# An expert loop on Trainium2: the next expert's input products formed between this one's output products

## The chip, the cores and the metric

The kernel runs on one core of one Trainium2 chip. The core has five engines that run by themselves and meet at semaphores: TensorE (PE, matrix products; PEld is its loading of the stationary operand), VectorE (DVE), ScalarE (ACT), GpSimd (POOL) and SyncE (SP, which here only issues transfers). The metric is device time in microseconds. Three timed runs of the kernel before gave 1420.69, 1421.56 and 1422.44 us; the median is 1421.56.

## What is computed

A decoder layer over 16 sequences of 256 tokens with 256 features: a state-space scan, an alignment with a second set of sequences, and a mixture of experts. Only the last matters here:

```python
gate_logits = jnp.einsum('te,ex->tx', x, gate_kernel)
weights, selected = jax.lax.top_k(gate_logits, TOP_K)      # 64 experts, 2 per token
...
h0 = jax.lax.ragged_dot(sorted_x, w0, group_sizes)         # 256 -> 512
h1 = jax.lax.ragged_dot(sorted_x, w1, group_sizes)         # 256 -> 512
inter = jax.nn.silu(h0) * h1
out_sorted = jax.lax.ragged_dot(inter, wo, group_sizes)    # 512 -> 256
```

4096 tokens times two choices are spread over 64 experts, each with 1.5 MB of float32 weights (w0, w1 and wo, 512 KB each).

## The kernel before

The kernel runs its stages one after the other: `states`, `wave`, `trace_back`, `expand` (which also routes the tokens), `experts` and `combine`. The change is in `experts` (line 1816) alone.

The experts are sorted by how many tokens they got. The 32 fullest are *wide*: they have room for 220 down to 134 tokens (`ROOM`, line 43), so two tiles of rows. The others are *narrow*, with room for 128. `TURN` (line 148) takes them in turns, wide, narrow, wide, and so on, 63 in all (`RANKS`); tokens that found no room, and the last expert, are served by a loop at the end (line 2003).

For expert k the work is, with m counting the four parts of 128 of the 512 hidden features:

- POOL gathers its tokens (`gather`), four experts ahead in a ring of four; PE turns them so that features lie on partitions (`turn`), and DVE copies that out of PSUM (`take_turned`, line 2042) into one of two buffers `xt`.
- PE forms part m of both input products in `h_ps[m]` (`up`, line 1942; for each of the two products two matmuls of 128 rows of features, and the float32 ones count double in the trace, so 8 records a part).
- ACT applies silu to the first (`activate`, line 2019), DVE multiplies by the second into `inter[m]` (`product`, line 2048).
- PE adds part m's share of the output product: `down` (line 1953) for a narrow expert, with 256 columns in 2 records; `down_wide` (line 1958) for a wide one, transposed, in 4 records of as many columns as tokens. For a wide expert ACT copies the result (line 2033), PE turns it back (`back`, line 1968) while it works on the next expert, and DVE takes it out (`take_out`, line 2055). POOL scatters the rows to DRAM (`scatter`).
- SP loads the weights of expert k + 4 into the slot of expert k as soon as the last output product of k is done (lines 1862 to 1864), in three transfers. Four slots (`WRING`) are there.

The order on each engine is written out by hand. On PE it is, for expert k: up 0, up 1, the turning back of the wide expert before, up 2, down 0, up 3, down 1, the turning of the tokens of k + 1, down 2, down 3 (lines 1979 to 1996). Then expert k + 1 begins. ACT does the four silus and, for a wide expert, the copy. DVE does the four products, with the taking out of the wide expert before between the second and third, then the copy of the turned tokens, then the taking out of a narrow expert.

Of the kernel before, what the change touches and what calls it, by code (L numbers as in the profile page):

```python
# [6 lines left out]
ACT = mybir.ActivationFunctionType  # L7
# [13 lines left out]
FC = F // P  # L21
# [17 lines left out]
WRING = 4  # L39
RANKS = E - 1  # L40
# [1775 lines left out]
def experts(K):  # L1816


    nc, sem = K.nc, K.sem
    XR = 4  # L1820
    with ExitStack() as c:
# [7 lines left out]
        ot = sb("mo_ot", [P, DC, 2 * P])  # L1829
# [5 lines left out]
        ot_ps = ps("mo_ot_ps", [P, DC, 2 * P])  # L1835
# [9 lines left out]
        room = [ROOM[r] for r in TURN]  # L1845
        wide = [r < WIDE for r in TURN]
# [80 lines left out]
        def _(pe):  # L1927
# [11 lines left out]
            def turn_static(k):  # L1939
                turn(k, k % XR, moved(k), room[k], wide[k])  # L1940
# [27 lines left out]
            def back(k):  # L1968
# [6 lines left out]
                                                ot[:, c_, a * P:a * P + n], K.ident[:, :])  # L1975
                m.then_inc(back_mm, 1)

            turn_static(0)
            for k in range(RANKS):
                r, n = k % WRING, room[k]  # L1980
                pe.wait_ge(K.w_in[r], (k // WRING + 1) * 48)
                go_down = down_wide if wide[k] else down
                up(k, r, k % 2, 0, n)
                up(k, r, k % 2, 1, n)
                if k >= 1 and wide[k - 1]:
                    back(k - 1)
                up(k, r, k % 2, 2, n)
                if not wide[k] and k >= 2:
                    pe.wait_ge(o_ok, k - 1)
                go_down(k, r, 0, n)  # L1990
                up(k, r, k % 2, 3, n)
                go_down(k, r, 1, n)
                if k + 1 < RANKS:
                    turn_static(k + 1)
                go_down(k, r, 2, n)
                go_down(k, r, 3, n)
                if k == RANKS - WRING + 1:
                    pe.wait_ge(down_mm, k * FC)
                    pe.sem_inc(done, 1)
            back(RANKS - 1)  # L2000
            n = late_count(pe)
            r = RANKS % WRING
            with pe.Fori(0, n) as g:
# [12 lines left out]
        @block.scalar  # L2016
        def _(act):

            def activate(k, m, n):
                act.wait_ge(up_mm, k * FC + (m + 1))  # L2020
                if not isinstance(k, int) or k >= 1:
                    act.wait_ge(inter_ok, k * FC + (m + 1 - FC))
                nc.scalar.activation(silu[m][:, 0:n], h_ps[m][:, 0, 0:n], ACT.Silu).then_inc(silu_ok, 1)  # L2023

            nc.scalar.preload_act_table(ACT.Silu)
            for k in range(RANKS):
                for m in range(FC):
                    activate(k, m, room[k])
                if wide[k]:
                    act.wait_ge(down_mm, k * FC + FC)  # L2030
                    if backs(k) > 1:
                        act.wait_ge(back_mm, backs(k) - 1)
                    nc.scalar.activation(ot[:, :, 0:room[k]], ot_ps[:, :, 0:room[k]], ACT.Copy).then_inc(ot_ok, 1)
            n = late_count(act)
            with act.Fori(0, n) as g:
                for m in range(FC):
                    activate(g + RANKS, m, P)

        @block.vector
        def _(dve):  # L2040
# [23 lines left out]
                m.then_inc(o_ok, 1)  # L2064

            take_turned(0, 0, room[0])
            for k in range(RANKS):
                for m in range(FC):
                    product(k, m, room[k])
                    if m == 1 and k >= 1 and wide[k - 1]:  # L2070
                        take_out(k - 1)
                if k + 1 < RANKS:
                    take_turned(k + 1, (k + 1) % 2, room[k + 1])
                if not wide[k]:
                    take_out(k)
            take_out(RANKS - 1)
            n = late_count(dve)
            with dve.Fori(0, n) as g:
                k = g + RANKS
# [134 lines left out]
```

## Time and profile before

| | us |
|---|---|
| median of three timed runs | 1421.56 |
| the profiled execution, timed | 1432.94 |
| its span | 1431.2 |
| PE busy | 986.7 (69% of the span) |
| DVE busy | 906.0 (63%) |
| POOL busy | 678.4 (47%) |
| ACT busy | 554.0 (39%) |

The span is cut into 40 slices of 35.8 us; the expert loop takes slices 27 to 38 or so. Busy time of PE holds the modelled length of every matmul, which in a stream overlaps the next, so a gap in PE is a little longer than its idle time. A group of the waits says which engine waited with which instruction, and what released it. SPq rows are transfers that SP issued.

### The profile page before, as it was taken

What the parts mean: (1) busy time and instruction counts of PE and PEld (TensorE: products, weight loads), DVE (VectorE), ACT (ScalarE), POOL (GpSimd) and SP (SyncE); (2) the same over time, 40 slices, a digit from 0 to 9 for tenths busy, and PEclk for the clock granted to TensorE, in tenths of its full rate; (3) what the DMA queues carried; (4) which work ended last, traced back from release to release, by engine and by line L of the source; (5) the groups of instructions that cost most, each with busy time, mean ns of one, the idle gap of its engine ahead of it and who ended that gap; (6) DMA issues with size and microseconds to landing.
All of it is one profiled execution on the core that took longest, in us unless ns stands there. A gap on an engine that the chain in (4) does not pass through costs nothing. (4 is left out here: it accounts for less than half of the span.)

```text
span 1431.2 us, 20102 instructions
## 1 busy us (share of the span) xinstructions
PE 986.7 (69%) x6433; PEld 893.7 (62%) x6433; DVE 906.0 (63%) x2024; ACT 554.0 (39%) x1236; POOL 678.4 (47%) x685
## 2 busy tenths in 40 slices
PE   3667778777788762677001675399999898989950
PEld 2566757767677651666001564399998888888850
DVE  1999999999999950888887765133323232323217
ACT  3668787786877650443000442021212121111110
POOL 5886887878778720000000677334343434444310
PEclk9989999999999985555555976599999999999985
DMA  6544545555465511122130111678788788778629
GB/s 199 180 142 139 172 139 181 157 160 181 138 183 163 167 41 38 19 41 37 22 115 34 45 45 31 204 239 268 263 271 261 258 268 265 263 252 267 220 67 349
DMA packets 171161, 231.99 MB, mean 162 GB/s; under 512 B 42172, under 2 KB 95788, under 8 KB 170352
## 3 DMA queue, kind: packets, MB, share of 16 engines
q1 hardware_dynamic: 152924, 207.06, 46.3%
q0 software_dynamic: 11280, 19.06, 4.0%
q10 hardware_dynamic: 6852, 4.57, 1.0%
q8 instruction: 52, 0.85, 0.2%
q14 instruction: 53, 0.43, 0.1%
HBM read 202.78 MB, written 23.65 MB: 158 GB/s over the span
## 5 line engine op out<-in xcount | busy, mean ns | idle before, releaser
L848 PE MATMUL st_y_ps<-ident,st_hc 128*128 128x128 f32 x2048 | 276.2, 293 | 114.2 <-DVE st_hc L491 114.1
L848 PEld LDWEIGHTS st_y_ps<-ident,st_hc 128*128 128x128 f32 x2048 | 258.5, 205 | 137.3 <-DVE st_hc L491 136.6
L373 POOL TENSOR_TENSOR st_u<-st_dx,codes 128x1024 f32<-128x1024 f32 x128 | 299.0, 2359 | 37.8 <-DVE st_h L483 37.2
L483 DVE TENSOR_TENSOR_SCAN st_h<-st_da,st_u 128x512 f32<-128x512 f32 x256 | 298.0, 1206 | 9.8 <-POOL st_u L373 9.6
L1949 PE MATMUL mo_h<-mo_xt,w 128*128 128x128 f32 (+17 forms) x2048 | 283.0, 290 | 1.8 <-DVE mo_xt L2046 1.0
L1949 PEld LDWEIGHTS mo_h<-mo_xt,w 128*128 128x128 f32 x2048 | 272.8, 194 | 6.3 <-issue 2.5
L2052 DVE TENSOR_TENSOR mo_inter<-mo_silu,mo_h 128x128 f32<-128x128 f32 (+17 forms) x256 | 75.0, 304 | 289.6 <-ACT mo_silu L2023 242.8
L1890 POOL DMA_INDIRECT outs<-mo_o,choice x95 | 93.7, 986 | 246.1 <-DVE mo_o L2063 233.9
L2023 ACT ACTIVATE mo_silu<-mo_h 128x128 f32<-128x128 f32 (+17 forms) x256 | 70.8, 290 | 327.7 <-PE mo_h L1949 227.1
L614 ACT ACTIVATE st_da<-st_delta,st_a_neg 128x510 f32<-128x510 f32 x256 | 171.7, 685 | 66.4 <-DVE st_h L483 59.6
L491 DVE TENSOR_TENSOR st_hc<-st_h,st_cps 128x1024 f32<-128x1024 f32 x128 | 152.9, 1195 | 0.0
L1083 PE MATMUL wv_e<-wv_r,wv_shift 128*128 128x1 f32 x274 | 75.8, 347 | 57.7 <-DVE wv_r L1021 57.3
L1883 POOL DMA_INDIRECT mo_xg<-xn,table x95 | 92.5, 974 | 37.6 <-issue 28.4
L1083 PEld LDWEIGHTS wv_e<-wv_r,wv_shift 128*128 128x128 f32 x274 | 68.5, 312 | 65.4 <-issue 63.9
L1963 PE MATMUL mo_ot_ps<-mo_inter,wo 128*128 128x190 f32 (+16 forms) x512 | 90.3, 310 | 23.5 <-DVE mo_inter L2052 16.2
L1963 PEld LDWEIGHTS mo_ot_ps<-mo_inter,wo 128*128 128x128 f32 x512 | 74.8, 193 | 31.4 <-DVE mo_inter L2052 21.6
L621 ACT ACTIVATE st_cps<-codes 128x512 f32<-128x512 f32 x128 | 76.6, 599 | 39.5 <-DVE st_hc L491 39.3
L1955 PE MATMUL mo_o_ps<-wo,mo_inter 128*128 128x256 f32 x256 | 73.9, 392 | 0.0
L1418 POOL DMA_INDIRECT bucket<-ex_row,ex_slot x64 | 63.1, 985 | 17.9 <-issue 17.8
L1073 ACT ACTIVATE wv_r<-wv_e,wv_edge_big 128x1 f32<-128x1 f32 x137 | 35.8, 261 | 64.7 <-PE wv_e L1083 64.7
L1147 POOL MEMSET tb_shift<- 128x128 f32 x1 | 0.2, 206 | 110.6 <-POOLq L910 110.6
L1686 ACT ACTIVATE ex_apart<-ex_col,ex_mid 128x256 f32<-128x256 f32 x32 | 14.2, 494 | 96.9 <-DVE ex_mid L1481 96.7
(300 smaller groups left out, 1332.9 us busy)
## 6 DMA issues: line engine op xcount, KB each, us to landing
codes<-bc SPq DMA_DIRECT2D x256, 256.0 KB, 3.9
w<-in_L_ffn_w_dram SPq DMA_DIRECT2D x128, 512.0 KB
wo<-in_L_ffn_wo_dram SPq DMA_DIRECT2D x64, 512.0 KB
co_got<-outs SPq DMA_DIRECT2D x16, 512.0 KB, 6.2
x<-in_x_dram SPq DMA_DIRECT2D x8, 512.0 KB, 8.9
st_cx<-in_ctx_dram SPq DMA_DIRECT2D x8, 512.0 KB, 4.4
dist<-st_dd SPq DMA_DIRECT2D x8, 512.0 KB, 5.2
codes<-wv_code SPq DMA_DIRECT2D x32, 128.0 KB, 3.4
```

The source lines that it names most:

```text
L373: nc.gpsimd.tensor_tensor(u_sb[k % URING][:, :, :], dx[p % 2][:, :, :], over_chunks(b_sb[k % BRING]), ALU.mult).then_inc(u_ok, 1)
L483: nc.vector.tensor_tensor_scan(h_sb[k % HRING][:, dh, :], da_ps[dh][:, :], u_sb[k % URING][:, dh, :], 0.0, ALU.mult, ALU.add).then_inc(h_o ...
L491: nc.vector.tensor_tensor(hc_sb[k % RING][:, :, :], h_sb[k % HRING][:, :, :], over_chunks(c_ps[k % 2][:, :]), ALU.mult).then_inc(hc_ok, 1)
L614: nc.scalar.activation(by_batch(da_ps[dh][:, :]), by_batch(delta[p % 2][:, dh, :]), ACT.Exp, scale=a_neg[:, dh, n:n + 1]).then_inc(da_ok, 1)
L621: nc.scalar.activation(c_ps[k % 2][:, :], c_sb[k % CRING], ACT.Copy).then_inc(c_ok, 1)
L848: m = nc.tensor.matmul(y_ps[t // 2][:, t % 2, dh * P:(dh + 1) * P], hc_sb[k % RING][:, dh, t * P:(t + 1) * P], K.ident[:, :], start=False, ...
L1083: nc.tensor.matmul(e_ps[t % 4][:, 0:1], K.shift[:, :], r[:, t + 1, SW:SW + 1], start=True, stop=True).then_inc(e_mm, 1)
L1883: nc.gpsimd.indirect_dma_start(xg[k % XR][0:n, a, :], None, K.xn_dram[:, :], bass.IndirectOffsetOnAxis(ap=K.table[0:n, at:at + 1], axis=0) ...
L1890: nc.gpsimd.indirect_dma_start(K.outs_dram[:, :], bass.IndirectOffsetOnAxis(ap=K.choice[0:n, at:at + 1], axis=0), o_sb[k % XR][0:n, a, :], ...
L1949: ins = nc.tensor.matmul(h_ps[m][:, i, 0:n], K.w[r][i][:, c_, m * P:(m + 1) * P], xt[u][:, c_, 0:n], start=(c_ == 0), stop=(c_ == DC - 1))
L1963: ins = nc.tensor.matmul(ot_ps[:, c_, 0:n], K.w[r][2][:, m, c_ * P:(c_ + 1) * P], inter[m][:, 0:n], start=(m == 0 and c_ == 0), stop=(m == ...
L2052: nc.vector.tensor_tensor(inter[m][:, 0:n], silu[m][:, 0:n], h_ps[m][:, 1, 0:n], ALU.mult).then_inc(inter_ok, 1)
```

## The change

PE works in iterations k = -1 to 62. In each it forms part m of the input products of expert k + 1, then part m of the output product of expert k, for m = 0 to 3. Behind m = 1 it turns back the wide expert k - 1, and behind m = 2 it turns the tokens of expert k + 2. ACT takes the transposed result of expert k - 2 ahead of the silus of expert k. DVE takes out a narrow expert k - 1 at the head of an iteration, then does the products of expert k + 1, with the taking out of a wide k - 1 behind m = 1 and the copy of the turned tokens of k + 2 behind m = 2. The slots of the weights stay four, and are freed as before by the last output product; the weights of expert k + 1 are now in use while those of k still are. The go-ahead for the weights of the last loop waits for the output products of expert 60.

```diff
+            def down_of(k, m):
+                if not wide[k] and m == 0 and k >= 2:
+                    pe.wait_ge(o_ok, k - 1)
+                (down_wide if wide[k] else down)(k, k % WRING, m, room[k])
+
             turn_static(0)
-            for k in range(RANKS):
-                r, n = k % WRING, room[k]
-                pe.wait_ge(K.w_in[r], (k // WRING + 1) * 48)
-                go_down = down_wide if wide[k] else down
-                up(k, r, k % 2, 0, n)
-                up(k, r, k % 2, 1, n)
-                if k >= 1 and wide[k - 1]:
-                    back(k - 1)
-                up(k, r, k % 2, 2, n)
-                if not wide[k] and k >= 2:
-                    pe.wait_ge(o_ok, k - 1)
-                go_down(k, r, 0, n)
-                up(k, r, k % 2, 3, n)
-                go_down(k, r, 1, n)
-                if k + 1 < RANKS:
-                    turn_static(k + 1)
-                go_down(k, r, 2, n)
-                go_down(k, r, 3, n)
+            for k in range(-1, RANKS):
+                after = k + 1
+                if after < RANKS:
+                    pe.wait_ge(K.w_in[after % WRING], (after // WRING + 1) * 48)
+                for m in range(FC):
+                    if after < RANKS:
+                        up(after, after % WRING, after % 2, m, room[after])
+                    if k >= 0:
+                        down_of(k, m)
+                    if m == 1 and k >= 1 and wide[k - 1]:
+                        back(k - 1)
+                    if m == 2 and after + 1 < RANKS:
+                        turn_static(after + 1)
                 if k == RANKS - WRING + 1:
-                    pe.wait_ge(down_mm, k * FC)
+                    pe.wait_ge(down_mm, k * FC + FC)
                     pe.sem_inc(done, 1)
-            back(RANKS - 1)
+            if wide[RANKS - 1]:
+                back(RANKS - 1)
...
-            for k in range(RANKS):
-                for m in range(FC):
-                    activate(k, m, room[k])
-                if wide[k]:
-                    act.wait_ge(down_mm, k * FC + FC)
-                    if backs(k) > 1:
-                        act.wait_ge(back_mm, backs(k) - 1)
-                    nc.scalar.activation(ot[:, :, 0:room[k]], ot_ps[:, :, 0:room[k]], ACT.Copy).then_inc(ot_ok, 1)
+
+            def take_transposed(k):
+                act.wait_ge(down_mm, k * FC + FC)
+                if backs(k) > 1:
+                    act.wait_ge(back_mm, backs(k) - 1)
+                nc.scalar.activation(ot[:, :, 0:room[k]], ot_ps[:, :, 0:room[k]], ACT.Copy).then_inc(ot_ok, 1)
+
+            for k in range(RANKS + 2):
+                if k >= 2 and wide[k - 2]:
+                    take_transposed(k - 2)
+                if k < RANKS:
+                    for m in range(FC):
+                        activate(k, m, room[k])
...
             take_turned(0, 0, room[0])
-            for k in range(RANKS):
+            for k in range(-1, RANKS + 1):
+                after = k + 1
+                if k >= 1 and not wide[k - 1]:
+                    take_out(k - 1)
                 for m in range(FC):
-                    product(k, m, room[k])
+                    if after < RANKS:
+                        product(after, m, room[after])
                     if m == 1 and k >= 1 and wide[k - 1]:
                         take_out(k - 1)
-                if k + 1 < RANKS:
-                    take_turned(k + 1, (k + 1) % 2, room[k + 1])
-                if not wide[k]:
-                    take_out(k)
-            take_out(RANKS - 1)
+                    if m == 2 and after + 1 < RANKS:
+                        take_turned(after + 1, (after + 1) % 2, room[after + 1])
```

## Rows read from the trace of the kernel before

**Rows 1.** The page's 40 slices of the span: PE's busy tenths

```profile
PE   3667778777788762677001675399999898989950
```

**Rows 2.** Busy time in windows (window, length, engines, clock, transfers' share, GB/s)

```profile
933.00:1372.00 439.00, 414.96 (x3034) 391.78 (x3033) 131.99 (x402) 81.71 (x279) 177.31 (x182) 0.99 0.78 256
933.00:947.00 14.00, 14.00 (x96) 13.59 (x95) 4.70 (x13) 2.56 (x9) 6.47 (x6) 1.00 0.81 262
1260.00:1276.00 16.00, 14.04 (x99) 13.34 (x98) 4.13 (x13) 2.45 (x9) 5.78 (x6) 0.89 0.72 232
```

**Rows 3.** Who waited for whom, 924.5 to 1372: total us, times, longest

```profile
DVE mo_inter L2052 <- ACT mo_silu L2023: 237.7, 187, 4.3
DVE mo_o L2063 <- PE mo_o_ps L1955: 17.2, 30, 0.6
PE mo_ot_ps L1963 <- DVE mo_inter L2052: 16.2, 19, 2.0
PE mo_ot_ps L1963 <- issue: 7.2, 11, 1.3
```

**Rows 4.** Order of time (start, us, instruction, idle before), wide expert at 1309.50, PE and ACT

```profile
1309.50 2.98 PE L1949 MATMUL mo_h<-mo_xt,w 128*128 128x138 f32 x24
1310.64 0.29 ACT L2023 ACTIVATE mo_silu<-mo_h 128x138 f32<-128x138 f32 x1 [2.59 <-issue]
1313.80 0.29 ACT L2023 ACTIVATE mo_silu<-mo_h 128x138 f32<-128x138 f32 x1 [2.88 <-PE mo_h L1949]
1315.27 0.46 ACT L2023 ACTIVATE mo_silu<-mo_h 128x138 f32<-128x138 f32 x2 [1.18 <-PE mo_h L1949]
1316.99 1.95 PE L1949 MATMUL mo_h<-mo_xt,w 128*128 128x128 f32 x16
1318.08 0.28 ACT L2023 ACTIVATE mo_silu<-mo_h 128x128 f32<-128x128 f32 x1 [0.49 <-PE mo_h L1949]
```

**Rows 5.** The same, the last experts, behind which no weights are loaded

```profile
1347.03 1.95 PE L1949 MATMUL mo_h<-mo_xt,w 128*128 128x128 f32 x16
1353.40 2.90 PE L1949 MATMUL mo_h<-mo_xt,w 128*128 128x134 f32 x24
1359.10 1.95 PE L1949 MATMUL mo_h<-mo_xt,w 128*128 128x128 f32 x16
1367.49 0.28 ACT L2023 ACTIVATE mo_silu<-mo_h 128x134 f32<-128x134 f32 x1 [0.63 <-PE mo_h L1949]
```

**Rows 6.** The same, SP: first transfers of the weights of one expert

```profile
1111.16 0.72 SPq L1813 DMA_DIRECT2D w<-in_L_ffn_w_dram  x2
1119.06 0.89 SPq L1813 DMA_DIRECT2D w<-in_L_ffn_w_dram  x2
1304.04 1.30 SPq L1813 DMA_DIRECT2D w<-in_L_ffn_w_dram  x2
1310.85 0.45 SPq L1813 DMA_DIRECT2D w<-in_L_ffn_w_dram  x2
1317.90 0.89 SPq L1813 DMA_DIRECT2D w<-in_L_ffn_w_dram  x2
```

**Rows 7.** The same, one more wide expert: issue, late silus, PE behind them

```profile
1266.89 1.47 SPq L1813 DMA_DIRECT2D w<-in_L_ffn_w_dram  x2
1271.25 0.65 ACT L2023 ACTIVATE mo_silu<-mo_h 128x140 f32<-128x140 f32 x3 [4.30 <-PE mo_h L1949]
1272.80 2.08 PE L1963 MATMUL mo_ot_ps<-mo_inter,wo 128*128 128x140 f32 x8
```

**Rows 8.** Transfers from 1104 to 1120 us, 40 slices of 0.4 us: busy tenths

```profile
DMA  0007257999998999647446599999999998200000
```

**Rows 9.** Order of time: single instructions whose lengths the sum uses

```profile
938.32 4.26 PE L1949 MATMUL mo_h<-mo_xt,w 128*128 128x200 f32 x24
1351.98 0.29 DVE L2052 TENSOR_TENSOR mo_inter<-mo_silu,mo_h 128x128 f32<-128x128 f32 x1 [1.04 <-ACT mo_silu L2023]
1352.54 0.44 DVE L2046 COPY mo_xt<-mo_xt_ps 128x268 f32<-128x268 f32 x1 [0.27 <-PE mo_xt_ps L1935]
```

## The prediction

> **What bounds the kernel now.** I read the page's 40 slices first [rows 1]: the expert loop is the stretch of roughly 925 to 1372 us, where TensorE (PE) stands at 8 to 9 tenths and above all the slices before. Outside it the change touches nothing. The table of that stretch [rows 2] says PE was busy 415.0 of 439 us, DVE 132, ACT 82, the transfers 0.78 of their time, at a granted clock of 0.99; in the first pairs it is 14.00 of 14 us. So PE is the bound and 24 us of idle time is all that the busy figure leaves. The list of PE's waits [rows 3] places that: 30 waits, 16.2 + 7.2 = 23.4 us, all ahead of an output product of a wide expert. They lie behind DVE's product, DVE lies behind ACT's silu (237.7 us, mostly harmless), and ACT behind PE by the order of time.
>
> That last step is the odd one, as the order of time shows [rows 4]. A wide expert starts on PE at 1309.50; its silu of part 0 starts on time (1310.64). Part 1 is formed by about 1311.6, yet its silu starts at 1313.80, and parts 2 and 3 at 1315.27. In the narrow expert behind it (input products from 1316.99) the first silu starts on time. In the last experts, when no more weights are loaded [rows 5], the wide expert's silus start on time too (part 1 at 1367.49, after 0.63 of idle time), and the two experts from 1347.03 to 1359.10 run without a PE wait. So a pair of wide and narrow expert takes 13.86 us between weight issues (1304.04 to 1317.90 [rows 6]), and 12.07 us (1347.03 to 1359.10 [rows 5]) without the stall, 0.16 of it from fewer columns. The stall is ACT's and goes with the weight issue: parts 2 and 3 were released 1315.27 - 1310.85 = 4.42 us behind the first issue, and 1271.25 - 1266.89 = 4.36 in another pair [rows 4, 6, 7]. At that point the load before it is still in transit; at a narrow expert's issue, 1119.06 - 1111.16 = 7.9 us later, it no longer is [rows 6, 8].
>
> **What the stalls cost in all.** The idle time is 23.4 us. Each of the 30 waits also hides the tail of the matmul before it: a 138-column matmul is drawn 0.3 us long but in a stream they follow at (2.98 - 0.28)/23 = 0.117 us, so 0.17 us each, 5 us together. Two of the long waits (2.0 us) are followed by a fall of the clock from 2.4 to 1.2 GHz [rows 7]: a window of 16 us has 0.89 granted [rows 2], so 1.76 us is lost; the second pair, at 1334, looks the same: 3.4 us together. Sum 32 us. This is the most that the change can win.
>
> **Part 1: PE's order.** Now up(k+1, m) and down(k, m) alternate. No matmul is added or removed, and a switch between the two kinds costs nothing where the input is there: the last pair has as many switches and no wait [rows 5]. PE's work of a pair stays 12.07 us. It is split otherwise. Iteration B (narrow expert's input products, wide one's output products): 32 x 0.111 (from 16 in 1.95 us) + 16 x 0.114 (24 in 2.90) + 4 transposes of the same 128 columns x 0.11 = 5.8 us. Iteration A (the reverse, with the back transposes): 12.07 - 5.8 = 6.25 us [rows 5].
>
> **Part 2: what ACT and DVE owe.** A product(k+1, m) is now due a whole iteration later, so a late silu of part 1 or 3 costs nothing; 5.8 us of PE's work covers it. This removes all 30 waits as they are today. What is late next is the copy of the turned tokens. It stands behind product(k+1, 2) in DVE's order, and up(k+2, 0) opens the next iteration with a wait on it. In B the weight issue comes 1310.85 - 1309.50 = 1.35 us behind the start, as now, because it waits for the narrow expert's last output product as now. If ACT is released 4.42 us later, the silu of part 2 starts at 5.77. Behind it come silu 0.28 [rows 4], product 0.29, copy 0.44 [rows 9] and some 0.2 of hand-offs (an estimate: silu 0 starts 0.04 behind the drawn end of its part): PE can start at 6.98, and has been ready at 5.8. That is 1.15 us for a pair at 134 to 148 columns; at 190 columns a matmul takes 0.162 us (24 of 200 columns in 4.26 us [rows 9], scaled), B lasts 3.56 + 2.59 + 0.44 = 6.6 us and 0.4 us is left. Fourteen pairs at 0.7 and sixteen at 1.1 give 27.4; in the first two wide experts PE waits nowhere today [rows 2], which leaves 26.5. Bounds for this unseen wait: zero if the release comes 1.15 us sooner, 2.2 us a pair if it comes 1 us later (POOL's last two gathers do, since the wide expert's result is now taken some 1 us deeper in the iteration). I take 1.15, the row's own distance. The gaps then stay under 1.2 us, below those that were followed by a fall of the clock, so its 3.4 us are not paid again.
>
> **Part 3: weights held longer.** Slot k is still freed by the last down of its expert, but up(k+4) comes one iteration sooner. The time from issue to need falls from three iterations, 18.1 - 1.35 = 16.7 us, to two, 12.07 - 1.35 = 10.7. A load takes 1117.8 - 1111.16 = 6.7 us, and with scatters between some 8 (from 1105 on; they thin out from 1110 to 1113) [rows 6, 8]: hidden, by 2.7 us. If that cover went, each microsecond more would cost 30 to 60 us over the loop. The gathers are due one iteration sooner as well; no PE wait in the loop is on one today [rows 3], they are issued three iterations ahead in POOL's order, and two are left: 0, and at worst a wait where POOL's last gather of a pair is late, which rival 3 takes in.
>
> **Part 4: edges.** The sooner input products of expert 0 and the later, bare output products of expert 62 are the same work in another place: 0. The late expert's weights are issued after expert 60 and have iteration 61 and the bare output products of 62, with what follows, some 10 us; hidden. One wait for the PE's own last product, at expert 60, drains PE once: 0.3 us. Two waits stand at new places: ACT's copy of a wide result heads its iteration, and silu 0, queued behind it, is due 0.9 us later (the copy takes some 0.4, as DVE's of as many elements [rows 9]); DVE's taking of a narrow result waits for the last output product (17.2 us in 30 waits today [rows 3]), and product 0 behind it is due an iteration later: 0 for both, up to 0.3 us a pair if the first is held by the stall.
>
> **Sum.** 32 removed, 26.5 + 0.3 returned: 5.2 us less. The profiled execution took 1432.94 us (span 1431.2), 11.4 above the median of 1421.56. Against its own time the forecast is 1427.7, for the median 1416.4.
>
> A rule of the Trainium skill (Perfetto Trace Analysis, section on TensorE's instruction lifecycle) says that a matmul's end in a profile is estimated from its size. By it the late silus could be PE's lateness, nothing would be removed, and the median would stay at 1421.6. The trace speaks against it: in the narrow expert and in the last wide one, the silus follow the drawn ends at once [rows 4, 5]; what chance is left to it is in rival 3.
>
> **The rivals.** (1) *The stall is absorbed.* The release follows something that no longer meets the part that matters: ACT is asked for parts 1 and 2 at some 2.2 and 3.6 us behind the start, with output products between, instead of 2.1 and 3.0. Then the 26.5 us are not returned. For it: the first wide experts, with wider parts and so ACT asked later, lose nothing [rows 2]. Against it: the release stood at 4.4 us in both pairs shown, and in those between. Time: 1421.6 - 32 = 1390; if all 11.4 us by which the profiled run is longer are such stalls, only 20.6 are there and it is 1401. I put 1396.
>
> (2) *Slower: the loads overlap in every iteration.* Today the issue of the narrow expert comes 7.9 us behind the previous one, with that load (6.7 us) done, and nothing stalls. In the new order A's issue (0.91 behind its start, 1317.90 - 1316.99 [rows 4, 6]) follows B's after 6.98 - 1.35 + 0.91 = 6.5 us, so it meets a load in transit too. Then ACT stalls in A as well: released at 0.91 + 4.42 = 5.3, the copy is there at 6.5 against 6.25, 0.3 us a pair, and up to 1 us if the backlog adds to it. 30 pairs: 10 to 30 us on top of the forecast, 1427 to 1446; I put 1433. It decides from the point where B's issue lies less than 6.7 us ahead of A's. For it: the sum above stands just on that side. Against it: ACT's copy of the wide result and the silu of part 0 come ahead of the stall. The skill's page DMA: Bandwidth & Descriptors (Issuing engines are not separate DMA queues) says that transfers issued from different engines share the same 16 and interleave; [rows 8] agrees, and by it denser iterations mean more overlap, so this rival's 1433.
>
> (3) *The change does not do what it says:* the silus are late by PE itself (below Sum), or PE waits for weights at the head of an iteration, since 0.78 of the transfers' time becomes 0.9 in a shorter pair. 1 us for every second expert is 30 us, of which the stall's own wait hides most: 1430. The first would be 1421.6.
>
> **How the numbers follow.** Forecast 0.42, rival 1 0.25, rival 2 0.25, rival 3 0.08. The forecast's own range is 1408 to 1424. About 0.2% (2.8 us) is what a measurement can tell here. Of the forecast's chance three quarters lie below 1418.7, of the rest most within 0.2%: faster 0.42 x 0.75 + 0.25 = 0.56, same 0.14 (0.08 of it from the forecast, 0.06 from rivals 2 and 3), slower 0.30. The range reaches into both outer cases: 1393 to 1437.
>
> **What would show it.** Right: no PE wait left in front of an output product; one wait of about 1.1 us in front of up(k+2, 0), every second iteration, released by DVE's copy (L2046's counterpart); pairs of about 13.2 us; the full clock from 935 to 1372. Part 3 right: no PE wait on a weight transfer. Rival 1: pairs of 12.1 to 12.5 us. Rival 2: such a wait in both iterations, and late silus behind both issues. Wrong altogether: pairs unchanged at 13.9 with PE waiting where it waits now.

## The result, and the profile after

The changed kernel takes 1435.28 us in the median of four runs (1432.3 to 1437.82), the kernel before 1421.12 beside it: a ratio of 1.009 (95% interval 1.0066 to 1.0114). It is slower by 14 us between the medians, some 13 by the ratio, where 5 us less were forecast. The number lies in the stated range (1393 to 1437), the sign is wrong.

Against [rows 1] PE's slices in the expert loop are no fuller, although the clock is now at its full 2.4 GHz all the time. The page of after, PE and its clock in 40 slices, and then the loop's stretch as in [rows 2]:

```profile
PE   3667778777788762777002665499999989898950
PEclk8889999999999985555555886699999999999985
```

```profile
933.00:1372.00 439.00, 404.90 (x2992) 381.49 (x2991) 126.74 (x397) 79.44 (x275) 176.72 (x182) 1.00 0.77 256
```

PE is busy for 405 of 439 us, 10 less than before. The list of waits (total us, times, longest) of the same stretch, for PE the answer to [rows 3]:

```profile
PE mo_h L1949 <- issue: 32.6, 28, 1.8
PE mo_ot_ps L1963 <- issue: 0.4, 1, 0.4
ACT mo_silu L2024 <- PE mo_h L1949: 307.6, 191, 4.7
```

The 30 waits ahead of an output product are gone but for one of 0.4 us, and 28 new ones stand ahead of an input product: 32.6 us for 23.4. Where they are is in the order of time of one iteration with narrow input products (start, us, instruction, idle before), the counterpart of [rows 4 and 6]:

```profile
1301.45 0.64 PE L1963 MATMUL mo_ot_ps<-mo_inter,wo 128*128 128x138 f32 x4
1301.55 1.53 SPq L1813 DMA_DIRECT2D w<-in_L_ffn_w_dram  x2
1305.22 0.90 POOL L1883 DMA_INDIRECT mo_xg<-xn,table  x1 [0.31 <-issue]
1305.91 0.28 ACT L2024 ACTIVATE mo_silu<-mo_h 128x128 f32<-128x128 f32 x1 [3.98 <-remote]
1307.41 0.62 DVE L2058 TENSOR_TENSOR mo_inter<-mo_silu,mo_h 128x128 f32<-128x128 f32 x2 [3.98 <-PE mo_ot_ps L1963]
1307.43 0.49 ACT L2024 ACTIVATE mo_silu<-mo_h 128x128 f32<-128x128 f32 x2 [1.25 <-PE mo_h L1949]
1307.94 0.44 DVE L2052 COPY mo_xt<-mo_xt_ps 128x276 f32<-128x276 f32 x1
1308.48 1.18 PE L1949 MATMUL mo_h<-mo_xt,w 128*128 128x138 f32 x8 [1.67 <-issue]
```

The silus of parts 2 and 3 start at 1307.43, DVE's product of part 2 behind the first of them, the copy of the turned tokens at 1307.94, and PE, idle for 1.67 us, at 1308.48. A pair takes 14.14 us (from 1294.34, the same place two experts before, to 1308.48), where 13.2 were forecast.

**When a kernel was run matters here.** Kernels sent together share a chip and the runs of the kernel before; call that a sitting. The kernel before took 1421.7, 1430.5 and 1429.9 us in three of the later sittings and 1395.7, 1396.8 and 1396.2 in three others, and within each all of its runs lie within 10 us. In the profiles of the second kind no silu starts more than 0.4 us behind the end of its part, in any kernel. I call them late and quiet sittings; the comparison that gave the result above was of the late kind. The chip alone does not decide it: sittings 2, 5 and 6 were on the same one, and 5 was quiet. Ratios below always are within a sitting; where times of two sittings are set side by side, the text says so.

| sitting | kernel before | runs of it |
|---|---|---|
| 1, quiet | 1395.74 | copy_early, no_loads, no_gathers, gathers_held |
| 2, late | 1421.72 | before_again, after_again, no_gathers_2, copy_early_2 |
| 3, quiet | 1396.84 | no_loads_2, gathers_held_2, before_held, early_and_held |
| 4, late | 1430.46 | no_loads_3, before_held_2 |
| 5, quiet | 1396.15 | gathers_held_3, after_third |
| 6, late | 1429.86 | extra_gather, gathers_held_4 |

### The profile page after: what moved, and what is told of

Its sections match the earlier page's. It is cut to its first block and busy times, and to the rows that moved or that the text cites. A ratio compares the mean times of both kernels' runs of the same rounds, so it can differ in the third digit from the quotient of the medians.

```text
span 1430.5 us, 20102 instructions
## 1 busy us (share of the span) xinstructions
PE 976.5 (68%) x6433; PEld 885.0 (62%) x6433; DVE 902.3 (63%) x2024; ACT 553.0 (39%) x1236; POOL 677.1 (47%) x685
## 5 line engine op out<-in xcount | busy, mean ns | idle before, releaser
L1949 PE MATMUL mo_h<-mo_xt,w 128*128 128x128 f32 (+17 forms) x2048 | 300.2, 290 | 34.8 <-issue 32.6
L373 POOL TENSOR_TENSOR st_u<-st_dx,codes 128x1024 f32<-128x1024 f32 x128 | 298.8, 2357 | 38.0 <-DVE st_h L483 37.4
```

The source lines that it names most:

```text
L373: nc.gpsimd.tensor_tensor(u_sb[k % URING][:, :, :], dx[p % 2][:, :, :], over_chunks(b_sb[k % BRING]), ALU.mult).then_inc(u_ok, 1)
L1949: ins = nc.tensor.matmul(h_ps[m][:, i, 0:n], K.w[r][i][:, c_, m * P:(m + 1) * P], xt[u][:, c_, 0:n], start=(c_ == 0), stop=(c_ == DC - 1))
```

## The experiments

My theory was still that of the prediction: ACT is released some time behind the issue of the weights (theory SP). The trace of after gave a rival. The release comes 1307.43 - 1301.55 = 5.88 us behind the first issue, where it was 4.42 before, but 1307.43 - 1305.22 = 2.21 us behind the start of POOL's last indirect transfer. In the kernel before, in sitting 2:

```profile
1219.85 0.89 POOL L1883 DMA_INDIRECT mo_xg<-xn,table  x1 [0.31 <-issue]
1222.06 0.47 ACT L2023 ACTIVATE mo_silu<-mo_h 128x144 f32<-128x144 f32 x2 [1.19 <-PE mo_h L1949]
```

This is 2.21 us too. The profile of before, which I had when I made the forecast, could have shown it. In the wide expert that starts at 1010.47 (start, us, instruction, idle before) SP issues the weights 1.4 us later than in most others, and the silus do not move with it:

```profile
1013.27 0.38 SPq L1813 DMA_DIRECT2D w<-in_L_ffn_w_dram  x2
1014.04 0.93 POOL L1883 DMA_INDIRECT mo_xg<-xn,table  x1 [0.30 <-issue]
1016.24 0.53 ACT L2023 ACTIVATE mo_silu<-mo_h 128x178 f32<-128x178 f32 x2 [2.58 <-PE mo_h L1949]
```

They come 2.97 us behind the issue instead of 4.4, and 2.20 behind the last gather. So the rival (theory POOL): the chain of gathers and scatters, each 1.3 us behind the other, holds ACT until it is over. In the texts below the times of an iteration count from the end of part 0's input product.

### The unchanged kernels

> The kernel before, unchanged, for a profile on the chip that runs the others. In the four runs so far (copy_early, no_loads, no_gathers, gathers_held) the kernel before took 1395.7 us, not 1421, and in their profiles no silu was late. If the late silus belong to the chip or to the moment and not to the kernel, a run at 1396 shows no PE wait ahead of the output products and pairs of 12.1 us; a run at 1421 shows the 30 waits and pairs of 13.9. If the kernel before still has its waits at 1396, the stall is a matter of the kernel's order and the theory falls.

> The changed kernel, unchanged. Where the kernel before takes 1396: no late silus, so there is nothing to win and nothing to give back, and the same matrix work: 1394 to 1397, ratio 0.998 to 1.001. Where the kernel before takes 1421: the wait for the copy of the turned tokens is back in every second iteration (1.8 us, 28 times), 1432 to 1437, ratio 1.008 to 1.011.

> The changed kernel, unchanged. Where the kernel before takes 1421 or more: 1432 to 1440, ratio 1.008 to 1.011 where it takes 1421, 1.003 to 1.006 where it takes 1430. Where the kernel before takes 1396 and no silu is late: there is nothing to win and nothing to give back, 1394 to 1398, ratio 0.998 to 1.002.

Sitting 2 was late: before_again took 1421.22 us (ratio 1.0, 0.9988 to 1.0013), after_again 1435.45 (1.0099, 1.0084 to 1.0114). Sitting 5 was quiet: after_third took 1397.23, ratio 1.0013 (0.9998 to 1.0029), no difference that this measurement can tell. Its narrow input products and silus in the same place of the loop, with the same chain on POOL:

```profile
1223.90 1.05 PE L1949 MATMUL mo_h<-mo_xt,w 128*128 128x128 f32 x8
1226.37 0.28 ACT L2024 ACTIVATE mo_silu<-mo_h 128x128 f32<-128x128 f32 x1 [1.10 <-PE mo_h L1949]
1227.75 0.28 ACT L2024 ACTIVATE mo_silu<-mo_h 128x128 f32<-128x128 f32 x1 [1.10 <-PE mo_h L1949]
1228.49 0.88 POOL L1883 DMA_INDIRECT mo_xg<-xn,table  x1 [0.30 <-issue]
1236.30 1.05 PE L1949 MATMUL mo_h<-mo_xt,w 128*128 128x128 f32 x8
```

The silus of parts 1 and 2 start at 1226.37 and 1227.75, before the last gather even begins, and a pair takes 12.40 us (1223.90 to 1236.30). The order of PE costs nothing and gives nothing where no silu is late. So the whole difference between the kernels is how each meets the late silus.

before_again also shows what the profile of before [rows 3] was: an execution with more of the stall than others. Its waits:

```profile
PE mo_ot_ps L1963 <- DVE mo_inter L2052: 10.7, 21, 1.1
PE mo_ot_ps L1963 <- issue: 4.8, 11, 0.6
```

15.5 us instead of 23.4, none longer than 1.1, and no fall of the clock in the loop; that execution took 1419.03 us.

### Without the loads, without the gathers

```diff
                 sp.wait_ge(down_mm, (k - WRING + 1) * FC)
-                load_weights(K, sp, expert_at(K, sp, k), k % WRING)
```

for no_loads, and for no_gathers

```diff
             def gather(k):
...
                 for a, at, n in tiles(k):
+                    if k >= XR:
+                        continue
```

with the waits for what is no longer transferred taken down to what the first four experts bring.

> The changed kernel without the loading of the weights of experts 4 to 62 (the four experts' weights loaded first are used again and again; the loop at the end still loads its own). Theory SP (the one of the prediction): the late silus come from the issue of the weights and from their transfer in transit. Then every silu starts 0.04 us behind its input product, the wait at the head of every second iteration is gone, and the time is about 1385. Theory POOL: the late silus are released some 2.2 us behind the start of POOL's last indirect transfer of its chain (3.60 + 2.21 after the change, 2.43 + 2.24 before it), whatever SP does. Then nothing changes: silus of part 2 at 5.8 us and 1432 to 1437. Theory both: the two have to meet; then 1385 as well.

> The changed kernel without the gathering of the tokens of experts 4 to 62 (the tokens of the first four are turned again and again; the loop at the end still gathers its own). POOL's chain in the iteration that stalls is then the one scatter at 1.0 us, without the gathers at -0.3, 2.3 and 3.6. Theory SP: silus of parts 1 and 2 stay as late as they are (4.3 and 5.8 us) since the weights are issued as before, 1432 to 1437. Theory POOL and theory both: the release follows the scatter by 1.8 to 2.2 us, so it is there by 3.2 us, the copy of the turned tokens by 4.5, and PE's wait vanishes: about 1385.

Sitting 1 was quiet, so these two told nothing of the stall: 1398.55 (ratio 1.0018, 1.0008 to 1.0029) and 1399.44 (1.0023, 1.0012 to 1.0033). Both were run again.

> The changed kernel without the gathering of the tokens of experts 4 to 62, as in no_gathers. It says something only where the kernel before takes 1421. There theory SP (the weights' issue and transfer) gives 1432 to 1437 with the silu of part 2 at 5.8 us; theory POOL (the chain of indirect transfers) and theory both give a release by 3.2 us and 1395 to 1400. Where the kernel before takes 1396: 1396 to 1400 as before.

> The changed kernel without the loading of the weights of experts 4 to 62, as in no_loads. It says something only where the kernel before takes about 1421. no_gathers_2 has shown there that without POOL's gathers the silus are on time (1395 us) though SP issues the same weights. Theory POOL alone (a chain of indirect transfers holds back ACT, whatever SP does): 1432 to 1437, silu of part 2 at 5.8 us. Theory both (the chain has to meet the issue of the weights): every silu 0.04 us behind its input product, 1394 to 1400. Where the kernel before takes 1396: 1396 to 1400 again.

> The changed kernel without the loading of the weights of experts 4 to 62, as in no_loads and no_loads_2, which both ran where the kernel before takes 1396 and no silu is late. It says something only where the kernel before takes about 1421. Theory POOL alone (a chain of indirect transfers holds back ACT, whatever SP does): 1432 to 1437, silu of part 2 at 5.8 us. Theory both (the chain has to meet the issue of the weights): every silu 0.04 us behind its input product, 1394 to 1400.

no_gathers_2, late sitting: 1395.17 us, ratio 0.9819 (0.9804 to 0.9834). The weights are issued as before, and the silus are on time (of the 256, seven are over 0.4 us late, and PE waits for none of them):

```profile
1208.53 0.84 SPq L1813 DMA_DIRECT2D w<-in_L_ffn_w_dram  x2
1208.81 0.98 POOL L1892 DMA_INDIRECT outs<-mo_o,choice  x1 [0.90 <-DVE mo_o L2071]
1209.62 0.28 ACT L2026 ACTIVATE mo_silu<-mo_h 128x128 f32<-128x128 f32 x1 [1.11 <-PE mo_h L1951]
1211.00 0.28 ACT L2026 ACTIVATE mo_silu<-mo_h 128x128 f32<-128x128 f32 x1 [1.11 <-PE mo_h L1951]
```

no_loads_2 fell on a quiet sitting (1396.59, ratio 0.9994). no_loads_3 did not: 1437.57 us, ratio 1.0046 (1.0025 to 1.0068), as slow as the changed kernel with its loads in another late sitting (1435.45). PE waits 28 times ahead of an input product, 34.6 us. Between 1243.5 and 1257 SP issues nothing, and:

```profile
1253.84 0.89 POOL L1882 DMA_INDIRECT mo_xg<-xn,table  x1 [0.30 <-issue]
1256.12 0.49 ACT L2023 ACTIVATE mo_silu<-mo_h 128x128 f32<-128x128 f32 x2 [1.94 <-PE mo_h L1948]
1257.18 1.21 PE L1948 MATMUL mo_h<-mo_xt,w 128*128 128x142 f32 x8 [1.62 <-issue]
```

2.28 us behind the last gather, with PE's wait behind it. The share of the transfers' time in the loop is 0.13 there. Theory SP falls, and so does "both have to meet": the gathers are needed for the late silus, the weights are not.

### The gathers held back

```diff
                 if k + XR < RANKS:
+                    if wide[k]:
+                        pool.wait_ge(down_mm, k * FC + FC)
                     gather(k + XR)
```

> The changed kernel, with one wait more on POOL: the two gathers of a wide expert are issued only when the last output product of the wide expert four before is done, that is at the head of the iteration with wide input products, where POOL idles now. Nothing is left out. Theory SP: the silus stay late in the same iteration, 1432 to 1437. Theory POOL: the last indirect transfer in the stalling iteration is now the scatter at 1.0 us, the release is at about 3.0, PE's wait goes there. In the other iteration POOL then has two gathers and two scatters, up to 5.8 us: if the chain alone makes the stall, it comes back there, with the copy at 6.5 to 7 against 6.3, 0.3 to 0.8 us a pair, 1395 to 1410. Theory both (the weights' issue has to meet the chain): the issue at the head of this iteration meets the two gathers too, so silus come late by 2.2 us behind the second gather; the pair still gets shorter, 1385 to 1400.

> The changed kernel with the wide expert's two gathers held back to the head of the next iteration, as in gathers_held. Nothing is left out. Where the kernel before takes about 1421: in the iteration with narrow input products the last indirect transfer is the scatter at about 1.0 us, the release at 2.9 or so, one silu late by 1.5 us, PE's wait gone there. In the other iteration the weights are issued from -1.3 to 0.1 us, and the two gathers start at about -1.2 and 0.1: theory both has silus late there until 2.3 us (one, by 0.8 us), which costs PE nothing; theory POOL alone has them late behind the whole chain of four, until about 6.8, and 0.5 to 1 us of a wait a pair comes back. So 1394 to 1402 by both, 1408 to 1425 by POOL alone. Where the kernel before takes 1396: 1395 again.

> The changed kernel with the wide expert's two gathers held back, as in gathers_held. no_loads_3 has shown that the weights' issue is not needed for the late silus, and before_held_2 that in the kernel before the held gathers bring 1396 where it takes 1430. Where the kernel before takes 1421 or more: the last indirect transfer of the iteration with narrow input products is the scatter at about 1.0 us, so the silus of parts 1 and 2 are released by 2.8 to 3.2 us, the copy of the turned tokens is there by 4.5, and PE waits nowhere: 1394 to 1400. If the release follows the length of the whole chain instead, the wait moves into the other iteration: 1408 to 1425. Where the kernel before takes 1396: 1395 to 1398 again.

> The changed kernel with the wide expert's two gathers held back, as in gathers_held. Where the kernel before takes 1421 or more: silus released by 2.8 to 3.2 us behind the scatter at 1.0, PE waits nowhere, 1394 to 1400; if the release follows the length of the whole chain, the wait moves into the other iteration: 1408 to 1425. Where the kernel before takes 1396: 1395 to 1398 again.

The first three fell on quiet sittings: 1395.18, 1398.2 and 1395.73 us, ratios 1.0002, 1.0005 and 1.0003, each with 1 in its interval. gathers_held_4 had a late one: 1395.63 us, ratio 0.9765 (0.9749 to 0.9782).

```profile
1209.92 0.28 ACT L2026 ACTIVATE mo_silu<-mo_h 128x128 f32<-128x128 f32 x1 [1.70 <-issue]
1210.14 0.98 POOL L1890 DMA_INDIRECT outs<-mo_o,choice  x1 [0.30 <-issue]
1212.17 0.45 ACT L2026 ACTIVATE mo_silu<-mo_h 128x128 f32<-128x128 f32 x2 [1.97 <-PE mo_h L1951]
```

The chain of that iteration now ends with a scatter at 1210.14, and the silus of parts 1 and 2 come 2.03 us behind it: still late, but soon enough for the copy, and PE does not wait. That the stall would come back in the other iteration, which has the two gathers and two scatters now, was expected of theory POOL alone (1408 to 1425) and did not happen: there every silu is on time. The four are not one chain there:

```profile
1203.57 0.89 POOL L1883 DMA_INDIRECT mo_xg<-xn,table  x1 [0.30 <-issue]
1206.34 1.02 POOL L1890 DMA_INDIRECT outs<-mo_o,choice  x1 [1.88 <-DVE mo_o L2071]
1207.66 0.86 POOL L1890 DMA_INDIRECT outs<-mo_o,choice  x1 [0.31 <-issue]
```

The second gather starts at 1203.57, and POOL is idle for 1.88 us before the first scatter. The unbroken chain begins with that scatter and goes on into the next iteration: 1206.34, 1207.66, 1208.83, 1210.14. The trace of after has the same pattern. There the chain has six members, from 1298.82 on in the iteration shown above. In its loop from 933 us on, none of the 47 parts whose input product ended during the first or second member had a silu over 0.4 us late, 5 of 31 during the third had, and all 71 from the fourth on. In the trace of before it is none of 34 up to the third, 16 of 46 during the fourth and 55 of 59 later. So the long delays stand late in an unbroken chain. The place in the chain goes with the kind of transfer and the part there, and no run varies its length by itself.

The same wait in the kernel before, with its own order on PE:

> The kernel before, with PE's, ACT's and DVE's order as they were, and the same one wait more on POOL: a wide expert's four-ahead gathers start when the last output product of the wide expert is done. Where the kernel before takes about 1421: in the wide expert's input products the last indirect transfer is then a scatter at -0.1 us instead of a gather at 2.4, the release at 1.8 instead of 4.6, the silu of part 1 late by under 1 us, and the 30 waits of PE vanish: 1395 to 1402, without any change in the order of PE. If the order of PE is needed as well, 1410 or more. Where it takes 1396: the same as it.

> The kernel before with the order of PE, ACT and DVE as it was, and one wait more on POOL, as in before_held. Where the kernel before takes about 1421: in the wide expert's input products the last indirect transfer is a scatter at -0.1 us instead of a gather at 2.4, the release at about 1.8 instead of 4.6, and the 30 waits of PE vanish: 1395 to 1402 without any change in the order of PE. In the narrow expert the gathers at -0.6 and 0.7 us now meet the issue of the weights; if the first silus of it are late by that, it is by under 2 us, and PE waits there for 0 to 1 us a pair, up to 1420. Where the kernel before takes 1396: the same as it.

In the quiet sitting 1396.61 (0.9996, 0.9979 to 1.0013); in the late one 1396.07, ratio 0.9764 (0.9742 to 0.9786).

```profile
1245.91 0.99 POOL L1890 DMA_INDIRECT outs<-mo_o,choice  x1 [0.30 <-issue]
1247.94 0.47 ACT L2025 ACTIVATE mo_silu<-mo_h 128x140 f32<-128x140 f32 x2 [1.62 <-PE mo_h L1951]
```

Again 2.03 us, and the 30 waits that the change was meant for are gone, but for one of 0.3 us, without the change. This version beats the kernel before in a late sitting (and the changed one, by the 1435 us of another such sitting) and equals the one before in a quiet one.

### The chain made longer

```diff
+                if k >= XR and wide[k]:
+                    if k > XR:
+                        pool.wait_ge(x_in[(k - 2) % XR], moved_in(k - 2))
+                    a, at, n = tiles(k)[0]
+                    nc.gpsimd.indirect_dma_start(spare[0:n, :], None, K.xn_dram[:, :],
+                                                 bass.IndirectOffsetOnAxis(ap=K.table[0:n, at:at + 1], axis=0)
+                                                 ).then_inc(x_in[k % XR], 16)
```

> The changed kernel with one gather more for every wide expert from the sixth on, behind its own two, into a tile that nobody reads. Nothing is left out. It doubles nothing but the suspected cause: the chain of indirect transfers ends 1.3 us later, at 4.9 instead of 3.6 us. Where the kernel before takes 1421 or more: if the release follows the last transfer by 2.2 us, the silu of part 2 moves from 5.8 to about 7.1 us, PE's wait from 1.8 to 3.1 us, and the time by 28 x 1.3 = 36 us, to 1468 to 1480. If the release follows something else (the start of the chain, the scatter, the weights), 1432 to 1440 as without it. Where the kernel before takes 1396: 1396 to 1400, since POOL has idle time for it.

The wait in it is for the gathers of two experts before; in the trace POOL does not stand at it, the transfers still follow each other by 1.2 to 1.3 us. Late sitting: 1511.05 us, ratio 1.0571 (1.0554 to 1.0589). Against the 1435.4 of after_again, in another late sitting, it is 76 us more, not 36; the forecast of 1468 to 1480 missed.

```profile
1311.41 0.99 POOL L1892 DMA_INDIRECT mo_spare<-xn,table  x1 [0.31 <-issue]
1313.97 0.49 ACT L2033 ACTIVATE mo_silu<-mo_h 128x128 f32<-128x128 f32 x2 [2.64 <-remote]
1315.04 2.23 PE L1958 MATMUL mo_h<-mo_xt,w 128*128 128x142 f32 x8 [3.07 <-issue]
```

The release moved with the chain: the gather added starts at 1311.41, the silu of part 2 2.56 us behind it, at 7.26 us of the iteration instead of 5.8. PE's waits went up as forecast, the first line for the input products:

```profile
PE mo_h L1958 <- issue: 68.4, 29, 3.2
PE mo_ot_ps L1972 <- issue: 5.7, 11, 0.8
```

That is 74.1 us against 33.0, 41 us more. The rest is TensorE's clock. The row above shows it: behind the gap of 3.07 us eight matmuls of 142 columns take 2.23 us, 1.13 at the full clock, and the stretch from 933 to 1450 us

```profile
933.00:1450.00 517.00, 442.48 (x2976) 414.92 (x2976) 125.53 (x394) 79.01 (x274) 201.26 (x208) 0.92 0.67 222
```

has 0.92 of the full clock granted: half speed for 0.16 of it costs at most 517 x 0.08 = 41 us. It costs less, because part of the slow time falls on PE's idle time. The stretch around the row above:

```profile
1314.50:1317.90 3.40, 2.86 (x10) 2.73 (x11) 0.63 (x3) 0.55 (x2) 0.00 (x0) 0.50 0.46 144
```

PE is busy for 2.86 of its 3.4 us. If the other slow stretches are like it, the clock costs 41 x 2.86 / 3.4 = 35 us (an estimate), and the two make the 76 that were measured. The waits of 1.8 us in the changed kernel were followed by no such fall (1.00), those of 2.0 us in the kernel before were, twice [rows 7]; here the clock stayed up behind one of 2.64 us (ahead of 1141.13, with 1.00 granted from 1141 to 1155).

### The copy ahead of the late silu

```diff
-                    if m == 2 and after + 1 < RANKS:
+                    if m == 0 and after + 1 < RANKS:
                         turn_static(after + 1)
...
-                    if m == 2 and after + 1 < RANKS:
+                    if m == 0 and after + 1 < RANKS:
                         take_turned(after + 1, (after + 1) % 2, room[after + 1])
```

> The changed kernel, with PE's turning of the next tokens and DVE's copy of them moved from behind part 2 to behind part 0. Nothing is left out. In the changed kernel PE waits 28 times, 32.6 us in all, at the head of an iteration for that copy, because it stands behind DVE's product of part 2 and this behind ACT's late silu of part 2 (released 5.8 us after part 0's input product). If that wait is the cost of the late silus and nothing else is late behind it, the wait vanishes: a pair takes 12.1 to 12.4 us instead of 14.1 and the time is 1435 - 28 x 1.8 = 1385 (1380 to 1392). If PE's late start is really something else (weights, gathers), it stays at 1430 to 1437. If the loads and gathers then limit the shorter pair, 1392 to 1415, with PE waits on a DMA.

> The changed kernel with the turning of the next tokens and DVE's copy of them behind part 0, as in copy_early. Where the kernel before takes 1421, the late silus are still there but nothing waits for them: 1396 to 1400, ratio 0.982 to 0.986 to the kernel before. Where it takes 1396: the same as it, as in copy_early.

> The changed kernel with both edits: the copy of the turned tokens behind part 0 (as in copy_early) and the two gathers held back (as in gathers_held). Where the kernel before takes about 1421: copy_early_2 alone gave 1401.8, no_gathers_2 1395.2; both edits together 1394 to 1400. Where it takes 1396: the same as it.

Quiet sitting: 1395.64, ratio 0.9994 (0.998 to 1.0009). Late sitting: 1401.84, ratio 0.9863 (0.9848 to 0.9878), a little above the 1396 to 1400 expected. The silus are as late as ever, and almost nothing waits for them:

```profile
1214.67 0.88 POOL L1883 DMA_INDIRECT mo_xg<-xn,table  x1 [0.31 <-issue]
1216.96 0.45 ACT L2024 ACTIVATE mo_silu<-mo_h 128x128 f32<-128x128 f32 x2 [1.25 <-PE mo_h L1949]
1216.08 1.37 PE L1949 MATMUL mo_h<-mo_xt,w 128*128 128x142 f32 x8
```

PE begins the next iteration at 1216.08, 0.88 us before the silu of part 2 that held it up in the changed kernel. PE's waits for the copy are down from 32.6 us to 2.4 in 8 waits. The time is still 6.7 us above that of no_gathers_2 in the same sitting; 2.4 of it are these, and the rest I have not placed. Both edits together were run in a quiet sitting alone: 1400.73, ratio 1.0032 (1.0014 to 1.0049), a little slower, where the same was expected. PE now turns tokens sooner that are gathered later, and waits for them, which is 2.8 of the 3.9 us:

```profile
PE mo_xt_ps L1937 <- DMA mo_xg<-xn,table: 2.8, 6, 0.7
```

## Why the prediction was wrong

**What held.** Part 1: no matrix work was added and its order costs nothing (after_third, 1.0013). Part 2: the 30 waits at the output products went (one of 0.4 us is left), and one wait ahead of up(k+2, 0), in every second iteration, behind DVE's copy, came in their place. The full clock from 933 to 1372 us: so it is. Part 3: no PE wait is on a weight transfer. Part 4: its waits are 0.3 to 0.5 us, once each. What failed is the cause of ACT's late release, and with it the size of the wait that the new order leaves.

**Two terms of the sum had the wrong size, both to the same side.**

*What is removed.* I took 32 us from the profiled execution, but set the forecast against the median by taking 11.4 off both sides, as if the extra length of that execution lay elsewhere. Most of it lay in the stall: in an execution of 1419.03 us, 13.9 less, the waits are 15.5 instead of 23.4, and the clock doesn't fall (3.4): 7.9 + 3.4 = 11.3 us. By these rows 32 - 11.4 = 20.6 of the median could be removed, which rival 1 had as a bound. The runs say somewhat more: in sitting 2, with the gathers left out and the silus on time, 1395.17 us stand beside 1421.72, which is 26.5, and the quiet sittings are 25 to 26 us below the late 1421. Some 5 us of it stand in none of the listed waits. Either way it is less than 32.

*What is returned.* I took the release to be 4.42 us behind the weights' issue, 5.77 us behind the start of the iteration, and so 1.15 us of waiting, on average 0.9. The release hangs on POOL's last indirect transfer instead, and comes 1307.43 - 1300.56 = 6.87 us behind the start of the iteration. It is 1.1 us later because POOL's chain begins with the wide expert's scatters, and they wait for its result, which the new order takes 1 us deeper in the iteration. I had named that shift and put it into a bound (2.2 us a pair) instead of the value. Measured are 32.6 us of waits, and 0.17 us of hidden tail for each: 28 x 0.17 = 4.8. Together 37.4 instead of 26.8. The runs of sitting 2 make it 1435.45 - 1395.17 = 40.3.

With both terms from the rows the same sum gives 1421.6 - 20.6 + 37.4 = 1438.4, against 1435.3 measured; with both from the runs of sitting 2, 1421.6 - 26.5 + 40.3 = 1435.4 (which closes by itself, since both are differences to one run). By the second pair 5.5 us of the forecast's error of 18.9 are the term removed and 13.5 the term returned. The second is the step that turned the sign.

**The cause behind the second term** was the step "the stall is ACT's and goes with the weight issue". In most wide experts of the profile of before the first weight issue and POOL's last gather stand 2.2 us from each other, and there the two candidates can't be told apart. In the one from 1010.47 they are 0.8 us apart, and the release keeps its distance to the gather (2.20), not to the issue (2.97). My other support, the last wide expert, without a weight issue before it [rows 5], has no gathers either, because both run four experts ahead. In the wide expert before it (1353.40) no weights are issued either, but POOL's chain is there up to a scatter at 1354.48, and the next silu starts 1.89 us behind that, some 1 us late. I looked for a cause among what *starts* near the stall, and had POOL's chain only as a contributor. It is the last member of the chain that the silu of part 2 follows in the rows shown, by 2.0 us behind a scatter and by 2.2 to 2.6 behind a gather, in seven kernels. It is not that ACT stands still until the chain is over: the silu of part 1 starts at 1305.91, 1.97 us behind the start of the last gather but one and before the last has ended. The rule of the Trainium skill (DMA: Bandwidth & Descriptors, Issuing engines are not separate DMA queues) was put beside rival 2 as a reason for lateness: with the shared engines almost empty (0.13) no_loads_3 is as late, so what it describes is not what holds ACT. [rows 8] shows how busy these engines were, not whose transfers they carried, so it bears less on that rule than I wrote.

**The rivals.** Rival 2 gave 1433, next to the result, for a reason that is not there: the silus of the iterations with wide input products are on time (1296.93, for a part formed at 1296.89), and the loads play no role. Rival 1, the stall absorbed, is what copy_early_2 shows to be possible in this order (1401.8), with one edit more. Rival 3 fell: neither PE nor weights made the silus late. A chance of 0.30 for slower was too small: the forecast's own mechanism gives a slower kernel from 20.6 / 30 = 0.7 us a pair on, and its bound went to 2.2. That 1435.3 lies inside the stated range is luck: the forecast's own range ended at 1424, and the rest up to 1437 was there for rival 2.

**What stays open.** Why a chain of indirect transfers on POOL releases ACT late at all, why only in some sittings, and why only from some length of an unbroken chain on. DVE and SP are held in the same stretches: the product of part 0 comes 1.2 us behind its silu, and the two issues at 1301.55 take 1.53 us instead of the 0.89 that those at 1294.27 and 1308.41 take. The Trainium skill (Perfetto Trace Analysis, the summary of the profiler's window by engine) says that a GpSimd transfer's record ends when its descriptors are made, not when the data has moved; the release falls 1.3 us behind such a record's end (1305.22 + 0.90 = 1306.12, then 1307.43), so it may go with the movement or with the signal of its end. No run here tells.

## What to carry to other kernels

Where a wait ends at the same time in every period, compare it with the last event of every queue, not with the first event of the nearest one, and look through all periods for one where two candidates are apart before you cost a reordering with either; here there was one. A reordering moves the stall's own cause too: here the result of a wide expert, and with it POOL's chain, came 1 us later. And set a profiled execution that is longer than the median against the terms of the sum first: here 11.3 of 13.9 us were in the very waits and clock falls that the sum counted.

## What the runs showed of the hardware

The kernel before takes 1421 to 1430 us in some sittings and 1396 in others, with the same matrix work; the 25 to 34 us go with late silus, which no profile of a quiet sitting has. One wait more on POOL, which starts two gathers some 4 us later, takes it to 1396 in a late sitting too (ratio 0.9764). A chain longer by one gather of 1.3 us cost 76 us in 30 pairs (between two late sittings), a little under half of it through the clock of TensorE, which stayed up behind the waits of up to 1.8 us in the changed kernel and fell to half behind the wait of 3.1 shown above.
